# Two fp4 networks of a fused eight-stage kernel: another order of rounding, scaling and second products

## The reference, cut to what matters

```python
def fp4_quant_dequant(x):                     # in blocks of 16 along the last dim
    scale = max(max(|xb|) / 6, 1e-12)
    idx = searchsorted(_MID, |xb / scale|)    # nearest of 0, .5, 1, 1.5, 2, 3, 4, 6
    return _GRID[idx] * sign(xb) * scale

def fp4_linear(x, w):
    return einsum('bsk,nk->bsn', fp4_quant_dequant(x), fp4_quant_dequant(w))

gate, y = fp4_linear(x, w_gate), fp4_linear(x, w_up)      # 128 -> 352
return fp4_linear(silu(gate) * y, w_down)                 # 352 -> 128
```

## Time and profile before

| What | Value |
|---|---|
| Median of 3 runs | 1058.72 us (1055.12 to 1060.01) |
| The profiled execution's own time | 1050.42 us |
| Its span | 1048.6 us |
| Busy over the span: PE, DVE, ACT, GpSimd | 920.4 (88%), 776.2 (74%), 409.8 (39%), 349.1 (33%) us |
| Mean granted TensorE clock | 0.947 of full speed |
| Chain that ended last, by engine | PE 57%, DVE 33%, issue 4% |

### The profile page before, as it was taken

One profiled execution on the slowest core, in us unless ns is written; L12 is line 12 of the kernel. 1 busy time (PEld: TensorE's weight loads), 2 busy tenths in 40 slices (PEclk: granted clock), 3 DMA queues, 4 the chain that ended last, 5 costly groups with the idle time before them and its releaser, 6 DMA issues.

```text
span 1048.6 us, 16651 instructions
## 1 busy us (share of the span) xinstructions
PE 920.4 (88%) x6134; PEld 525.5 (50%) x6156; DVE 776.2 (74%) x1837; ACT 409.8 (39%) x678; POOL 349.1 (33%) x446
## 2 busy tenths in 40 slices
PE   7889999999999978889999985798999888988686
PEld 3434444443443555553534441555657456767454
DVE  5678888767667477787586579757665997788984
ACT  2435556554324344343433357132231334332232
POOL 6372323222213353322333320322121344343333
PEclk9899999999999998889999997699999899998887
DMA  5362122211000000000000000000000000000000
GB/s 135 106 182 78 48 69 60 72 35 72 1 1 1 1 1 1 1 1 1 1 0 1 1 1 0 3 1 1 1 1 2 1 1 1 2 2 3 0 11 30
DMA packets 11532, 24.34 MB, mean 23 GB/s; under 512 B 1323, under 2 KB 7635, under 8 KB 11315
## 3 DMA queue, kind: packets, MB, share of 16 engines
q1 hardware_dynamic: 11152, 22.30, 7.3%
q10 hardware_dynamic: 294, 0.91, 0.3%
HBM read 15.69 MB, written 7.34 MB: 22 GB/s over the span
## 4 chain that ended last, share of the span: by engine, by line
PE 57%; DVE 33%; issue 4%; POOL 2%; ACT 2%; DMA 1%; DVEq 0%; SPq 0%; POOLq 0%; ACTq 0%
PE ps L1065 5%; PE ps L1072 4%; PE ps L1060 4%; PE ps L419 3%; PE ps L369 3%; DVE XN L166 2%; PE ps L2122 2%; DVE a_MN L549 2%; PE ps L2119 2%; PE ps L389 2%; DVE g_C L1878 2%; PE ps L2725 2%; PE ps L945 2%; PE ps L1084 1%; PE ps L1045 1%
## 5 line engine op out<-in xcount | busy, mean ns | idle before, releaser
L549 DVE TENSOR_REDUCE a_MN<-ps 128x1 f32<-128x384 f32 (+3 forms) x154 | 93.2, 637 | 24.3 <-PE ps L372 22.7
L1288 POOL TENSOR_TENSOR f_Y<-f_Y,f_TT 128x512 f32<-128x512 f32 x48 | 60.9, 1269 | 131.9 <-DVE f_TT L1144 131.9
L1236 ACT ACTIVATE f_HH<-ps,pack_zero 128x512 f32<-128x512 f32 x64 | 44.0, 687 | 95.9 <-PE ps L1060 95.9
L119 POOL TENSOR_TENSOR rs<-t,mhalf 128x4 f32<-128x4 f32 x36 | 37.1, 1031 | 130.7 <-DVE t L102 129.2
L673 ACT ACTIVATE a_PT<-ps 128x1024 f32<-128x1024 f32 x56 | 57.3, 1024 | 57.4 <-PE ps L389 57.2
L1144 DVE SCALAR_TENSOR_TENSOR f_TT<-ps,pack_zero,f_X 128x512 f32<-128x512 f32 x64 | 47.8, 747 | 33.5 <-PE ps L1072 33.1
L1065 PE MATMUL ps<-f_XS,pack_zero 128*128 128x512 f32 x128 | 72.0, 645 | 0.0
L1072 PE MATMUL ps<-f_HH,pack_zero 128*128 128x512 f32 x128 | 65.8, 595 | 5.0 <-DVE f_TT L1144 5.0
L1060 PE MATMUL ps<-f_XS,pack_zero 128*128 128x512 f32 x128 | 67.3, 607 | 0.7 <-DVE f_XS L1028 0.7
L369 PE MATMUL ps<-a_KS,a_QS 72*128 72x128 bf16 (+3 forms) x224 | 53.8, 303 | 9.0 <-DVE a_MN L549 8.0
L1028 DVE TENSOR_TENSOR f_XS<-ps,XNT 128x512 f32<-128x512 f32 x64 | 43.7, 685 | 17.1 <-PE ps L945 15.0
(11 more groups left out here) (336 smaller groups left out, 2206.0 us busy)
## 6 DMA issues: line engine op xcount, KB each, us to landing
scratch<-a_parts SPq DMA_DIRECT2D x16, 384.0 KB, 3.7
a_QS<-scratch SPq DMA_DIRECT2D x14, 288.0 KB
a_KS<-scratch SPq DMA_DIRECT2D x42, 96.0 KB
pack_one<-in_one SPq DMA_DIRECT2D x1, 2694.5 KB, 9.3
pack_zero<-in_zero SPq DMA_DIRECT2D x3, 884.5 KB, 4.6
X<-in_x SPq DMA_DIRECT2D x4, 256.0 KB, 10.0
out_x<-X SPq DMA_DIRECT2D x4, 256.0 KB, 2.1
a_QS<-a_MT SPq DMA_DIRECT2D x42, 4.0 KB
```

Source lines behind the costliest of these rows:

```text
L549: dve.tensor_reduce(M.a_MN[:, n % 2, ti, h0:h0 + k], bank(M, M.bank["a_max", n, jj], 128 * (ti + 1) * k).rearrange("p (a c) -> p a c", a=k ...
L1288: pool.tensor_tensor(M.f_Y[:, i, :], M.f_Y[:, i, :], M.f_TT[:, u % 3, :], ALU.add).then_inc(made.sem, made.tick(n, u))
```

## The change

Stage 5 and 7 alone. DVE does in pass u: rate of u, rounding of u-1, bits of u, then the work of other stages, and the residual. GpSimd: product of u, then scaling of u-1. PE: `down(u - 2)`. ACT: silu of u, exact step of u-1, copies of u-2. In stage 7 the rounding of unit 7 stands behind the residual of pass 8, and its scaling is done by DVE instead of GpSimd. The useless products ahead of units 6 and 7 of stage 7 go.

```diff
@@ -2462,7 +2462,7 @@
             M.freed[2 * k + s] = (S[done], (n, t))
 
 
-FILL = {5: (8, 5, 2, 5, 2, 0, 0, 0), 7: (8, 4, 2, 2, 2, 2, 3, 2)}
+FILL = {5: (8, 5, 2, 5, 2, 0, 0, 0), 7: (8, 4, 2, 2, 2, 2, 0, 0)}
 
 
 def quant_ffn_tensor(pe, S, M, n):
@@ -2472,7 +2472,8 @@
 
         turned, tiles = S["q_turned"], (2 * u, 2 * u + 1)
         filler(pe, M, 4, FILL[n][u])
-        pe.wait_ge(S["q_hq"].sem, S["q_hq"].at(n, u))
+        done = S["q_round"] if (n, u) == (7, 7) else S["q_hq"]
+        pe.wait_ge(done.sem, done.at(n, u))
         for t in tiles:
             x = 4 + t % 2
             take(pe, M, x)
@@ -2504,8 +2505,8 @@
             quant_up_tensor(pe, S, M, n, u)
         if u == 2 and n == 7:
             retention_product(pe, S, M, 3, 7)
-        if u >= 3:
-            down(u - 3)
+        if 2 <= u < 10:
+            down(u - 2)
         if n == 5:
             if u == 6:
                 turn_tensor(pe, S, M, 6, 0, 5, M.XN, (S["normed"], (7, 0)))
@@ -2535,8 +2536,6 @@
     dve.wait_ge(made.sem, made.n)
     largest(dve, S, flat(M.q_HH, i), M.q_A[:, i, :])
     rate(dve, S, M.q_A[:, i, :], M.q_R[:, i, :], S["q_rate"], n, u)
-    if u:
-        quant_bits(dve, S, M, n, u - 1)
 
 
 def quant_bits(dve, S, M, n, u):
@@ -2547,7 +2546,14 @@
 def quant_ffn_vector(dve, S, M, n):
     def grid(u):
         dve.wait_ge(S["q_step"].sem, S["q_step"].at(n, u))
-        rounded(dve, S, M.q_V[:, u % 4, :], M.q_E[:, u % 4, :], S["q_round"], n, u)
+        if (n, u) != (7, 7):
+            rounded(dve, S, M.q_V[:, u % 4, :], M.q_E[:, u % 4, :], S["q_round"], n, u)
+            return
+        v, made = S["vec"], S["q_round"]
+        rounded(dve, S, M.q_V[:, u % 4, :], M.q_E[:, u % 4, :], v)
+        dve.wait_ge(S["q_turned"].sem, S["q_turned"].at(n, 2 * (u - 4) + 1))
+        dve.wait_ge(v.sem, v.n)
+        dve.tensor_tensor(flat(M.q_HQ, u % 4), blocks(M.q_V[:, u % 4, :]), wide16(M.q_A[:, u % 4, :]), ALU.mult).then_inc(made.sem, made.tick(n, u))
 
     def leave(b):
         residual(dve, S, M, n, b, 6 + b % 2, S["result"])
@@ -2558,13 +2564,15 @@
         if u == 8:
             if n == 5:
                 retention_factors(dve, S, M, 0)
-            quant_bits(dve, S, M, n, 7)
-            grid(6)
-            if n == 5:
+                grid(7)
                 norm_back(dve, S, M, 7, 1, M.X, M.XN)
                 retention_weighted(dve, S, M, 0)
         elif u < 8 and (n == 5 or u):
             quant_up_vector(dve, S, M, n, u)
+        if 1 <= u < 8:
+            grid(u - 1)
+        if u < 8:
+            quant_bits(dve, S, M, n, u)
         if n == 5:
             if u == 1:
                 norm_back(dve, S, M, 6, 3, M.X, M.XN)
@@ -2588,12 +2596,10 @@
                 quant_powers(dve, S, M, 7, 3)
             elif u == 5:
                 quant_back(dve, S, M, 7, 3)
-        if 2 <= u < 8:
-            grid(u - 2)
-        elif u == 8:
-            grid(7)
         if u >= 4 and u % 2 == 0:
             leave(u // 2 - 2)
+        if u == 8 and n == 7:
+            grid(7)
         if n == 5:
             if u == 5:
                 norm_back(dve, S, M, 7, 0, M.X, M.XN)
@@ -2633,12 +2639,12 @@
             turn_scalar(act, S, M, 7, 2)
         if u < 8 and (n == 5 or u):
             quant_up_scalar(act, S, M, n, u)
-        if u >= 3:
-            down(u - 3)
+        if 1 <= u <= 8:
+            exact(u - 1)
+        if 2 <= u < 10:
+            down(u - 2)
         if u == 8 and n == 5:
             retention_shares(act, S, M, 0)
-        if 1 <= u <= 8:
-            exact(u - 1)
         if n == 5:
             if u == 3:
                 quant_steps(act, S, M, 5, 3)
@@ -2669,14 +2675,12 @@
         pool.tensor_tensor(flat(M.q_HQ, u % 4), blocks(M.q_V[:, u % 4, :]), wide16(M.q_A[:, u % 4, :]), ALU.mult).then_inc(made.sem, made.tick(n, u))
 
     for u in range(11):
+        if u < 8 and (n == 5 or u):
+            quant_scaled(pool, S, M, n, u)
+        if 1 <= u < 8 or u == 8 and n == 5:
+            scale(u - 1)
         if u == 2 and n == 7:
             norm_root(pool, S, M, 8, 3)
-        if 2 <= u <= 8:
-            scale(u - 2)
-        if u == 8:
-            scale(7)
-        if u < 8 and (n == 5 or u):
-            quant_scaled(pool, S, M, n, u)
         if u == (2 if n == 5 else 3):
             quant_divide(pool, S, M, n, 3)
         if n == 5:
```

## The result

The changed kernel takes 1082.62 us (median of 4 runs, 1078.49 to 1087.14) against 1057.3 for the kernel before (4 runs, 1055.12 to 1060.01): ratio 1.0244, 95% interval 1.0208 to 1.028. It is 25.3 us slower, where 16 to 17 were forecast: half as much again, and 1 us beyond the top of the stated range (1083 on the 1058.72 before, +24.3). The profiled execution took 1080.52 (span 1078.5), before 1050.42 (1048.6).

What follows compares the result with a forecast made beforehand. DVE's own order was taken to set the pace until the last pass, then a chain through GpSimd, DVE, ACT and PE. First network +6 and second +11 gave 17 us, 1075 us, range 1060 to 1083.

Steps and rivals of the forecast that it cites:

- the hold: Rounding pairs, passes 1 to 7 of both networks: L1712 stands still for GpSimd's product, 1.07 us each (bounds 0 and 1.4).
- the collision doesn't decide: Rival: GpSimd's release comes behind L1712's issue, so nothing is held and the shorter tail gains; 1052 us, chance 0.10.
- half of it: Rival: extra waits fall into DVE's existing waits and the tail returns the rest; within 0.5%, 1059 us, chance 0.06.
- the hold for GpSimd's whole length: Rival: DVE is held for all of GpSimd's instruction, 3.16 us a pair; 3.6 more, 1079 us, chance 0.03.
- I take +6, bounds 3 and 9: First network: net delay in us after added holds, collisions that go away and time returned at the retention's start.
- The 7.6 of my sum: Whole first network: 16.7 us of added terms less 9.1 that goes away.
- about 1.5 to the retention's start: First network's end: down(7) no longer lies in pass 10, which returns about 1.5 us.
- nothing at full rate: Second products two passes behind, ACT's exact step ahead of its copies: no cost, since PE has room.
- the way to the last rate: Second network: the last rate comes 15.6 us later, or 17.9 if the second round trip too runs at half rate.
- PE's clock stays high: Rival: second round trip and tail at full rate; 6 + 8.4 = 14 us, 1073 us, chance 0.15.
- The tail: Last rate to the end: 21.3 us before, T+14.1 at full rate or T+17.4 at half; gives back 7.2 or 3.9.
- PE low nearly throughout: Rival: products of passes 5 to 7 also at the low clock; some 6 us more, 1081 us, chance 0.12.

Runs made afterwards that it cites:

- prod_writes: Changed kernel with GpSimd's product alone replaced by a write of a constant, the scaling still reading; 1067.76 us, 1.0118 of the kernel before.
- s5_only: New order in stage 5 (first network) alone, stage 7 in the old order; 1067.08 us, 1.0095 of the kernel before.
- leave_first: Changed kernel with the first network's last residual one pass earlier, in pass 9; 1074.99 us, 1.0176 of the kernel before.
- before_moves: Kernel before with two layer-norm parts of stage 5 (L166) moved to where GpSimd is idle; 1053.03 us, 0.9983 of the kernel before.
- s7_only: New order in stage 7 (second network) alone, stage 5 in the old order; 1070.79 us, 1.0121 of the kernel before.
- tail_parts: Kernel before with the last scaling on DVE and without the fillers of units 6 and 7 of stage 7; 1058.77 us, 1.0004 of the kernel before.
- fill_holes: Changed kernel with more filler products where PE stood; 1073.43 us, 1.0155 of the kernel before.
- after_writes: Changed kernel with GpSimd's product and scaling both replaced by writes of a constant; 1055.1 us, 0.9994 of the kernel before.

## Where the forecast held, and which step failed

*Right: the hold.* L1712 in all 7 passes of each network at 1957 ns, L2666 at 1962, the input's L1699 and L1710 at 1.60 and 1.87, L1672 at 0.19, all as forecast. 14 x 1.07 = 15.0, and prod_writes gives 14.8 back. Of the rivals, "the collision doesn't decide" and "half of it" fall with that. So does the hold for GpSimd's whole length: the pair at 833.36 ends at 836.23, 2.87 us, not 3.16. The rule of the Trainium skill's "SBUF — State Buffer", section "Who interferes with whom", that a GpSimd instruction which only writes does not contend with two-input DVE instructions, agrees with the runs with writes: the product's write ran its 0.69 us beside L1710 (0.88), and neither was longer.

*Failed: the step "I take +6, bounds 3 and 9" for the first network.* It measured 13.1 up to the retention's first block (12.2 over three traces of each order), and s5_only puts its share of the time at 10.1. It falls into three parts.

Up to the last pair the network was 9.9 later than at its start: 2.3 of rounding 5 and bits 6 moved ahead, and 7.6 of holds and waits. By my terms these would be about 6.9 there; the wait of 1.20 in pass 4 was not among them. (The 7.6 of my sum was for the whole network and agrees by chance: it had 1.3 for L1710 of pass 8 behind scaling 6, and that L1710 ran in 0.88, since two products that read PSUM lay between.)

Up to the last residual it was still 10.0, where I had 6.1. I took work that is only moved ahead to be made up by the stage's end, and the end to return "about 1.5 to the retention's start" besides. Neither came, for that residual stands behind PE's chain and behind other work of DVE.

From the last residual to the retention's first block another 3.1 came in (40.15 us for 37.08), which my sum had at nothing. PE in order of time (idle before it, by whom):
```profile
882.24 1.18 PE L2482 MATMUL ps<-pack_first,q_HQ 128*128 128x128 f32 x6 [3.49 <-POOL q_HQ L2675]
883.50 2.78 PE L2491 MATMUL ps<-pack_one,q_HT 128*128 128x128 f32 x12
...
889.03 1.61 PE L2491 MATMUL ps<-pack_one,q_HT 128*128 128x128 f32 x12 [0.30 <-ACT q_HT L2629]
...
896.25 0.76 PE L2847 MATMUL ps<-pack_zero 128*128 128x128 f32 x2 [3.38 <-DVE X L197]
896.95 3.10 PE L2729 MATMUL ps<-pack_zero,r_KM 32*128 32x128 f32 x32
```
PE stands 3.49 us for the scaling of unit 6, runs its second products at half rate (2.78), and finishes unit 7's at 890.6. DVE's masks wait for PE (1.74), norm_back follows, and only then the residual on which the retention waits (3.38). And PE, which had stood 3.38 us, then runs the first block at the lower level. The 32 matmuls take 3.10 us where the kernel before has them at 1.72, after a wait of 0.88:
```profile
882.71 0.46 PE L2843 MATMUL ps<-pack_zero 128*128 128x128 f32 x2 [0.88 <-DVE X L197]
883.10 1.72 PE L2725 MATMUL ps<-pack_zero,r_KM 32*128 32x128 f32 x32
```
The granted clock is 0.62 in 896 to 905 and was 1.00 in 882 to 891. So PE's rate accounts for these 3.1 of the 13.1, by a hole that the late residual makes, and not for the first 10. I had put the second products' new place at "nothing at full rate" and never walked PE's chain across the border between the stages. leave_first puts the residual 4.7 us earlier and takes 3.9 off the 13.1. No run fills the hole of 3.38 with products, so the 3.1 rests on the rows alone.

*Somewhat short: the way to the last rate.* Forecast 15.6, or 17.9 with the second round trip at half rate; it was 19.3. The turned input and its first products on PE:
```profile
1023.05 1.12 PE L181 MATMUL ps<-pack_first,XM 128*128 128x128 f32 x4 [5.33 <-DVE XM L1746]
1024.85 4.86 PE L2461 MATMUL ps<-pack_one,XNT 128*128 128x352 f32 x8 [0.69 <-ACT XNT L189]
...
1039.70 2.93 PE L2491 MATMUL ps<-pack_one,q_HT 128*128 128x128 f32 x12 [2.06 <-ACT q_HT L2629]
...
1047.66 1.11 PE L181 MATMUL ps<-pack_first,XM 128*128 128x128 f32 x4 [4.34 <-DVE XM L1746]
1049.46 4.50 PE L2461 MATMUL ps<-pack_one,XNT 128*128 128x352 f32 x8 [0.69 <-ACT XNT L189]
...
1056.86 2.54 PE L2461 MATMUL ps<-pack_one,XNT 128*128 128x352 f32 x8
```
Both trips run at the lower level (eight first products in 4.86 and 4.50 us; at the full rate 2.54), so the second takes 6.5 us (1047.60, the end of L1746, to 1054.07) instead of the 4.15 of rows 7. PE stood 5.33 and 4.34 us ahead of them, where I had said "some 7". With that the rival "PE's clock stays high" falls. DVE's waits, 994 to the end (total, times, longest):
```profile
DVE q_HH L2533 <- PE ps L2461: 9.5, 5, 4.7
DVE X L197 <- PE ps L2491: 5.0, 1, 5.0
```
Before the first products 9.5 us are waited where it was 2.8. The remaining 1.4 over my 17.9 holds two waits ahead of L2533 that I hadn't: 0.62 for PE in pass 3 (1014.18), and 0.71 in pass 5 (1038.29) for ACT's silu behind the held L1699, as in pass 4 of the first network.

*The tail, in part by luck.* DVE in the last pass:
```profile
1063.01 0.19 DVE L1676 TENSOR_SCALAR q_R<-q_R 128x44 f32<-128x44 f32 x1
...
1067.44 0.97 DVE L1710 SCALAR_TENSOR_TENSOR q_V<-q_E,q_V 128x704 f32<-128x704 f32 x1 [0.42 <-ACT q_E L1704]
...
1069.44 0.89 DVE L2556 TENSOR_TENSOR q_HQ<-q_V,q_A 128x704 f32<-128x704 f32 x1
1075.30 0.69 DVE L197 TENSOR_TENSOR X<-ps,X 128x512 f32<-128x512 f32 x1 [4.96 <-PE ps L2491]
```
From the last rate to the end 15.3 us for 21.3: 6.0 back, between my 3.9 and 7.2. But 21.3 is the tail of one trace. The same tail took 18.9 in s5_only and before_moves, where the second products of unit 6 ran in 1.58 instead of 2.90; against these the new one gives back 3.6. The new tail is steady: 15.3 in s7_only and leave_first too. The last scaling took 0.89 and was done at 1070.33, PE came to unit 7's transposes at 1072.11, so it bought nothing; in the old order tail_parts says the same.

*The sum.* 17 forecast against 26.4 (13.1 + 19.3 - 6.0) in the profile: 7.1 of the difference in the first network and the retention's start (3.9 up to the last residual, 3.1 behind it), 2.3 in the last network. Of the measured 25.3, the rivals' nearest was "PE low nearly throughout", 1081; but it isn't the cause: of the three sets of second products in passes 5 to 7 only one ran at the lower level (2.93, then 1.58 and 1.61), the first products of passes 5 and 7 took 2.54, and fill_holes had the clock up and still lost the first network's 10 up to the last residual.

## What to carry to other kernels

Release a GpSimd instruction that reads SBUF only where DVE's next instructions read PSUM or reduce; behind its release, each chain of two-input DVE instructions pays about 1.07 us here, and one for one where DVE sets the pace, however early its operands are ready. Where a stage's last residual starts the next stage, walk the chain of TensorE across the border, and don't count a shift inside the stage as given back. Work pulled out of a hole leaves the hole: first ask what DVE will do while a round trip through PE and ACT runs, and whether PE keeps its rate meanwhile.

## What the runs showed of the hardware

- The hold has the same size each time. 14 of 14 L1712 took 1957 ns (within 2 ns), and GpSimd's product 1962. GpSimd took its turn between two DVE instructions that follow each other without a gap; in none of the 14 did L1712 get in behind L1710 first.
- It ends before the recorded end of the other's row. L1712 loses 1.07 to an instruction that lasts 1.39 alone; from GpSimd's start at about 834.09 (833.52 + 1.96 - 1.39) DVE is on again after 1.25.
- Size doesn't protect: a tensor_scalar of 32 columns was held, 0.65 for 0.18 us.
- A GpSimd write of 128 x 704 takes 0.69 us, also beside a two-input L1710, which stays at 0.88 (after_writes, prod_writes). Beside a tensor_scalar it is held, to 1.00 (median of 15), and holds the next one in turn (0.98 for 0.42).
- The same code ahead of the first network reached its end up to 10.4 us apart in the sixteen traces (810.46 to 820.84 at the last residual before it). The first network with the retention's start differed by 2.7 us (105.6 to 108.3) with the same code, the rest by 3.5 (126.2 to 129.7). A difference of two single traces below that says little, unless it is taken between near landmarks where both traces show the same waits but one, as the 7.14 of prod_writes.
